# Row scatters issued in pairs with a wait between pairs, in a one-core block of mixture-of-experts and retention layers

## The reference, cut to what matters

```
x = x + 0.5 * ffn(layernorm(x))      # round 0
x = x + retention(layernorm(x))
x = x + 0.5 * ffn(layernorm(x))      # round 1, same weights

def ffn(x):
    x = x + softmax_attention(layernorm(x)) @ w_o + b_o      # 16 heads of 8
    h = layernorm(x)                                         # one row per token
    topv, topi = top_k(h @ gate_w + gate_b, 2)               # 2 of 8 experts for each token
    hid = relu(h @ W1[e] + b1[e]);  out_e = hid @ W2[e] + b2[e]
    return x + sum over the two experts of weight * out_e
```

## Time and profile before

| | |
|---|---|
| time, median of 3 runs | 750.09 us (747.48 to 752.07) |
| span of the profiled execution | 819.1 us |
| busy share of the span | PE 84%, PE weight load 66%, DVE 66%, ACT 59%, POOL 44% |
| chain that ended last, by engine | PE 59%, DVE 12%, ACT 11%, issue 8%, POOL 2%, DMA 2% |
| DMA, all queues | 56.67 MB, mean 69 GB/s |
| DMA packets of the queue that POOL feeds | 4544 packets, 9.84 MB, 3.6% of the 16 engines' span |
| granted TensorE clock, mean | 0.892 of full speed |

### The profile page before, as it was taken

How to read it: one execution, slowest core, us unless ns; L and a number is a source line. 1 busy time by engine, 2 the same in 40 slices (tenths; PEclk the granted TensorE clock), 3 DMA queues, 4 the chain that set the end, 5 groups by cost and what they waited for, 6 DMA issues and landing times.

```text
span 819.1 us, 17972 instructions
## 1 busy us (share of the span) xinstructions
PE 690.5 (84%) x5632; PEld 538.7 (66%) x5632; DVE 538.3 (66%) x1565; ACT 480.1 (59%) x1043; POOL 357.3 (44%) x493
## 2 busy tenths in 40 slices
PE   5999997877769948899999989899999768667991
PEld 3455555546759947799988987645555435667990
DVE  4779786852635437988988895778878566433333
ACT  3677775633438844566666646577677354435774
POOL 6501114423455450667667675521021543354541
PEclk9799999867969978999999999889999687787996
DMA  8980000013212133222221110320000001022215
GB/s 290 412 277 1 2 1 30 13 51 106 57 60 77 52 100 68 62 52 54 53 52 30 34 43 1 140 94 1 2 1 5 26 30 48 26 68 71 74 37 164
DMA packets 32108, 56.67 MB, mean 69 GB/s; under 512 B 5744, under 2 KB 23024, under 8 KB 31568
## 3 DMA queue, kind: packets, MB, share of 16 engines
q1 hardware_dynamic: 27472, 45.67, 18.5%
q0 software_dynamic: 4544, 9.84, 3.6%
HBM read 36.22 MB, written 22.01 MB: 71 GB/s over the span
## 4 chain that ended last, share of the span: by engine, by line
PE 59%; DVE 12%; ACT 11%; issue 8%; another core or an unknown queue 5%; POOL 2%; DMA 2%; DVEq 0%; SPq 0%; POOLq 0%; ACTq 0%
PE ps L1868 8%; PE ps L1883 8%; PE ps L1634 7%; PE ps L1616 5%; ACT pt L1389 5%; PE ps L1964 5%; PE ps L1574 3%; PE ps L1985 3%; DVE msp L779 2%; PE ps L1935 2%; PE ps L1562 2%; PE ps L1998 2%; PE ps L1969 2%; PE ps L2000 1%
## 5 line engine op out<-in xcount | busy, mean ns | idle before, releaser
L1389 ACT ACTIVATE pt<-ps 128x1024 f32<-128x1024 f32 x128 | 131.0, 1023 | 60.1 <-PE ps L1616 58.1
L779 DVE TENSOR_REDUCE msp<-ps 128x4 f32<-128x1024 f32 x128 | 150.4, 1218 | 4.0 <-PE ps L1599 3.7
L1452 ACT ACTIVATE hid<-ps,ws 128x128 f32<-128x128 f32 x312 | 89.1, 371 | 42.0 <-PE ps L1868 22.5
L652 POOL DMA_INDIRECT os<-osb,xt x78 | 75.9, 974 | 79.8 <-DVE osb L1112 69.7
L1883 PE MATMUL ps<-wpack,hid 128*128 x624 | 91.3, 293 | 12.7 <-ACT hid L1452 11.7
L1868 PE MATMUL ps<-hTe,ws 128*128 128x128 f32 x624 | 90.4, 292 | 8.8 <-ACT hTe L1443 6.8
L1883 PEld LDWEIGHTS ps<-wpack,hid 128*128 128x128 f32 x624 | 83.2, 207 | 15.6 <-issue 15.6
L1868 PEld LDWEIGHTS ps<-hTe,ws 128*128 128x128 f32 x624 | 83.0, 207 | 10.0 <-ACT hTe L1443 7.5
L644 POOL DMA_INDIRECT xs<-rows,sidx x64 | 62.6, 979 | 51.2 <-DVE sidx L1023 33.1
L1616 PE MATMUL ps<-qm,kp 32*128 32x256 f32 x512 | 70.3, 354 | 16.9 <-ACT pt L1389 9.6
L1616 PEld LDWEIGHTS ps<-qm,kp 32*128 32x128 f32 x512 | 44.1, 209 | 57.9 <-ACT pt L1389 33.0
(11 more groups left out here) (196 smaller groups left out, 1572.4 us busy)
## 6 DMA issues: line engine op xcount, KB each, us to landing
xs<-in_c_blank SPq DMA_DIRECT2D x1, 10872.0 KB, 43.6
wpack<-in_wmoe SPq DMA_DIRECT2D x2, 4112.0 KB, 13.7
xt<-xs SPq DMA_DIRECT2D x78, 72.0 KB
swap<-qr SPq DMA_DIRECT2D x32, 128.0 KB, 2.3
swap<-kr SPq DMA_DIRECT2D x32, 128.0 KB, 2.3
rows<-os SPq DMA_DIRECT2D x8, 256.0 KB, 3.8
xt<-os SPq DMA_DIRECT2D x8, 256.0 KB, 5.2
decay<-in_c_decay SPq DMA_DIRECT2D x1, 1536.0 KB, 10.3
```

What stands on the lines that cost most here:

```text
L652: e.indirect_dma_start(os_d, bass.IndirectOffsetOnAxis(ap=xt[:, k % XRING, D:D + 1].bitcast(U32), axis=0), osb[:, k % 8, :], None).then_in ...
L779: e.tensor_reduce(msp[:, s % 2, :, 64 * pr + AUG:64 * pr + AUG + 33:32].rearrange("p q j -> p j q"), ps[:, score_banks(2 * s + pr), :].rea ...
L1389: e.activation(pt[:, u % 4, :, :], ps[:, 2:4, :], ACT.Exp, scale=float(DK) ** -0.5).then_inc(f["pexp"].sem, 1)
L1452: e.activation(hid[:, t % 2, i, :], ps[:, t % 2, i * P:(i + 1) * P], ACT.Relu, bias=ws[:, k % 4, WB1 + i:WB1 + i + 1]).then_inc(m["hid"].s ...
```

## The change

One line is added in `PoolMoe.scatter`. Before each tile's two copies POOL waits on the semaphore of its own group: at tile i until it stands at `16 * 2 * i` above the value that the earlier groups of this parity have brought, that is until all earlier pairs of the group have landed. At tile 0 this is no wait for groups 0 and 1, and for a later group it waits for the group two before it.

More of the change, by code:

```diff
@@ L642, in scatter @@
                 for i in range(CT):
+                    wait_earlier(e, scattered[n % 2], n // 2, 16 * 2 * i)
                     for k in range(2):
```

## The result

The changed kernel takes 768.79 us (median of 4 runs, 766.85 to 769.86), the kernel before in the same comparison 748.79 us (746.70 to 752.07). The ratio is 1.023, with a 95% interval from 1.017 to 1.029: slower by about 2%. Forecast was no change, 746 to 756.

The account below looks back on a forecast made before the run. PE was taken to set the pace, with POOL behind it. Of 8 x 3.75 = 30 us on POOL, 0 reach the path: 819.1 + 0 for the profiled execution, so the median before, 750 us, range 746 to 756.

Parts of the forecast that it names:

- The price of the change: On POOL between scatter pairs: one wait costs 1.25 us, a group 3.75 us, all eight groups 30 us of idle time.
- The upper bound of 7.1: Highest price of a group's waits on POOL, 7.1 us, from SP's first page load 3.34 us after a scatter's start.
- The estimate from the Trainium skill: For the scatter waits: about 2.0 us plus bytes a DMA, read as wholly added, 3 x 2.0 = 6 us a group.
- What hides the 3.75 us, group by group: At all eight scatter groups: existing idle time or slack covers the added waits, so 0 us reach the path.
- Group 0: POOL idles 9.02 us until DVE's statistics are there; 5.3 us are left after the waits, the tightest cover on POOL.
- Group 1: POOL's next work waits 11.64 us for ACT; SP's first page load moves to 174.8, using 3.75 of 9.2 us slack.
- Group 2: SP's wait before stage 1 is ended by page numbers; POOL's idle time before its next work is 10.29 us in round 1.
- Group 3: Among the output stores: 2.1 us vanish in SP's page-number wait, 1.6 us delay stage 2's load, wanted 12.1 us after issue.
- Rival 1: At the scatter groups: waits cost more than their cover, from 3.0 us added a wait; at 5 us, 789 us; chance 0.07.
- Rival 2: At group 3: DVE's weight copies hold up POOL's descriptors; at 2.5 us a scatter, 774 us; chance 0.02.
- Rival 3: On PE: granted clock falls otherwise, 1.6 us a stretch; chance of more than 1%: 0.02 faster, 0.02 slower.
- Rival 4: Around the scatters: a gain, as something else gets faster with at most two in flight; no row seen; chance 0.01.

Follow-up runs that it names:

- 750 level: Occasions on which the kernel before the change takes about 750 us, all of its timed runs of one occasion alike.
- only0b: Against the changed kernel, waits kept in groups 0 and 4 alone, second sending; 753.57 us, ratio 1.0004 to the kernel before.
- only3b: Against the changed kernel, waits kept in groups 3 and 7 alone, second sending; 764.71 us, ratio 1.0161 to the kernel before.
- 817 level: Occasions on which the kernel before the change takes about 817 us; the trace in front of the prediction (span 819.1) lies with them.
- paired_c: The changed kernel without edit, timed again beside the kernel before at 816.75 us; 788.97 us, ratio 0.9682.
- the single edits: Against the changed kernel, waits kept in one of a round's four groups alone; first sending 806.98, 815.38, 807.34 and 816.50 us, kernel before 819.76.

## Why the prediction was wrong

**The price of the change was right.** Forecast 1.25 us a wait, from a landing of 2.23 us and a restart of 0.28. The changed kernel shows 2.56 - 1.26 = 1.30 in group 0, and its first trace adds 3.8 to 4.1 us to six of the groups, 4.6 to group 3 and 6.0 to group 2, in all 34.0 where the forecast had 30. The upper bound of 7.1 was not needed.

The estimate from the Trainium skill ("DMA: Bandwidth & Descriptors", Anatomy of one DMA) was 6 us a group; the measured times, near 3.8 us in most groups, decide for the rows.

**The step that failed is the cover: "What hides the 3.75 us, group by group".** Each cover there was read from a trace in which PE, ACT and DVE are held up by late semaphores at every group, by waits of which the longest at a group takes 3.87 to 8.55 us, while POOL works on. Such a stall puts everyone else behind POOL, and it looks like idle time of POOL. Without it:

- Group 0: 9.02 us of idle time forecast, 1.54 on the 750 level. Some 2.3 us are left over, and 1.5 in round 1 (2.33 us of idle time); only0b shows 0.3 us in place of the 3.8 (up to 2.7 by its interval), so part of that was absorbed further on, where is not shown.
- Group 1: 9.2 us of slack for the first page forecast, 5.5 there (171.14 - 163.72 - 1.9).
- Group 2: 10.3 us forecast from round 1, 3.56 in round 0. There the changed kernel also had a landing of 4.17 us where others take 2.3, beside SP's load of the retention weights issued at 182.40; in round 1, which has no such load, no landing of the twin group is that long. SP's timeline has it so:

```profile
182.40 0.34 SPq L470 DMA_DIRECT2D rw_in<-in_rw  x1
```

The landing in the chain of the changed kernel:

```profile
185.27 4.17 DMA xs<-rows,sidx
```

- Group 3: 12.1 us forecast, none there. On the 750 level the page numbers are written at 209.5 and the group's last scatter lands at 212.83 + 3.37 = 216.2, so SP waits for the scatters and not, as forecast, for the page numbers. This group and its twin in round 1 made 12.1 us. The landing in the chain of the kernel before on that level:

```profile
212.83 3.37 DMA xs<-rows,sidx
```

In the changed kernel PE stands still for that page and restarts slowly, as in only3b:

```profile
228.12 0.47 PE L1861 MATMUL ps<-ident,xt 128*128 128x128 f32 x1 [5.34 <-DMA xt<-xs]
228.38 1.92 PE L1869 MATMUL ps<-hTe,ws 128*128 128x128 f32 x8
```

**The warning was in the text and was sized wrongly.** The prediction noted that the trace was 9.2% longer than the median, and let every cover shrink by that share. The 72 us were not spread evenly. Some twenty waits of "remote" stood at the very groups that the change touches, and 5% of the chain, some 41 us, was under "another core or an unknown queue". PE was also busy 31.8 us longer for the same instructions (690.5 against 658.7), at a mean granted clock of 0.892 in place of 0.944; how much of that lay on the path is not worked out. The bracket "<-remote" even stands in a row that the prediction used.

**The rivals.** Rival 1 had the right consequence, an overflow of the covers, but put it down to dearer waits, with 3.0 us a wait as the point from which it decides; most waits cost 1.3 and the covers were small. Rival 2, DVE holding up descriptors, didn't occur: the scatters take 0.96 us as before. Rival 3, the clock, was taken as independent of the change, and came as its consequence, 2.6 us in round 0 and 1.7 in round 1 of only3b. Rival 4, a gain, had a chance of 0.01 and no row; on the 817 level it is real, 26 us, and the rows for it were the remote waits.

**The signs.** The prediction said that no wait of PE for a page would appear and that it was wrong if a transposing PE waited for a DMA. That sign came, 12.0 us in five waits in the changed kernel. The same waits of the kernel before on the 750 level (total us, times, longest us):

```profile
PE ps L1860 <- DMA xt<-xs: 1.9, 2, 1.6
```

**The forecast of no change is wrong on both levels**: for the 750 level by a loss of 17 to 20 us, and for the very level of the trace by a gain of 26.

## What to carry to other kernels

Before reading slack from a trace, compare its span with the timed runs, and when they differ by more than a per cent or two, find where the difference sits: a cover next to a stall of unknown origin is not a cover. A queue of fixed work that feeds other engines' loads has to be followed to the consumer that waits for it, and a long pause of PE must be priced with the lower clock that follows it. An added wait can also pay, where a long row of DMAs holds up others; that has to be measured on each kind of occasion on which the kernel will run.

## What the runs showed of the hardware

On the 817 level, ACT and DVE went on some microseconds after PE's product had ended by the profile (6.0 us at group 1 of the trace before, 4.4 in the row of paired_c) while POOL sent indirect DMAs one behind the other, and the groups sent in pairs with a wait between them had no such wait. I call that a late semaphore; the profile has the start of the waiting instruction, not the semaphore's way, and it models the ends of matmuls. Why it is late, no run here shows. It is a correlation over groups, with the single edits and all groups but 3 and 7 as its test, and no more of the mechanism than that.

What decides the level is open too: the two traces of the kernel before have the same instructions, bytes and packets (17972, 56.67 MB, 32108). Two of the six occasions of the experiments had the 817 level. Each occasion had one chip of the machine. Chips 3, 5 and 4, the last one twice, had the 750 level, chips 1 and 11 the 817 level. No chip showed both. So the level may belong to the chip and not to the occasion; no run tests that, and for the trace before no chip is on record.

After a pause of 5.35 us PE's granted clock was 0.53 over the next 7 us; after 1.64 us it stayed at 1.00.
